# Two attention layers and an MLP on one core: order of SyncE's transfers, lag of the transposed scores, and halves of a projection in the first layer

## What is computed

```python
q = einsum('oc,bct->bot', Wq, x) + bq      # x, kv: (8, 256, 512); 16 heads of 16
k = einsum('oc,bct->bot', Wk, kv) + bk
v = einsum('oc,bct->bot', Wv, kv) + bv
attn = einsum('bhqd,bhdk->bhqk', q * scale, k)          # 512 x 512 for each head
attn = softmax(where(kv_mask, attn, -inf))
mean = attn @ v
std = sqrt(relu(attn @ (v * v) - mean * mean))
out = (instance_norm(x) * std + mean) * mask
```

## Time and profile before

| | |
|---|---|
| median of 3 runs | 1814.33 us (1808.19 to 1818.41) |
| the profiled execution | 1805.06 us, span 1803.3 us |
| TensorE matmuls | 1657.7 us busy, 92% |
| VectorE | 1279.9 us, 71% |
| ScalarE | 1065.6 us, 59% |
| GpSimd | 342.6 us, 19% |
| costliest group on VectorE | L598, 256 x 1222 ns |
| costliest group on ScalarE | L770, 256 x 1024 ns |

### The profile page before, as it was taken

How to read it: one execution, slowest core, us unless ns; L and a number is a source line. 1 busy time by engine, 2 the same in 40 slices (tenths; PEclk the granted TensorE clock), 3 DMA queues, 4 the chain that set the end, 5 groups by cost and what they waited for, 6 DMA issues and landing times.

```text
span 1803.3 us, 30832 instructions
## 1 busy us (share of the span) xinstructions
PE 1657.7 (92%) x10589; PEld 1124.1 (62%) x10589; DVE 1279.9 (71%) x2758; ACT 1065.6 (59%) x2351; POOL 342.6 (19%) x435
## 2 busy tenths in 40 slices
PE   6988888898888888899999989999999899999999
PEld 3333333333333334788878877888888788888888
DVE  2766867777777765798999889999999763232322
ACT  1556666666665565777877878888878752121111
POOL 0001111302111123232232222233322130000000
PEclk8999999999999999899999999999999899999999
DMA  5444453444444332233223434333333340000000
GB/s 181 138 137 136 143 153 96 144 119 137 122 125 140 112 123 69 84 74 81 69 68 102 113 87 124 89 89 89 92 93 83 88 129 13 1 24 1 24 17 19
DMA packets 108891, 167.97 MB, mean 93 GB/s; under 512 B 23616, under 2 KB 39360, under 8 KB 108608
## 3 DMA queue, kind: packets, MB, share of 16 engines
q1 hardware_dynamic: 96720, 140.74, 27.4%
q0 software_dynamic: 9472, 20.99, 4.6%
q10 hardware_dynamic: 2544, 4.26, 0.8%
HBM read 72.06 MB, written 34.60 MB: 59 GB/s over the span
## 4 chain that ended last, share of the span: by engine, by line
PE 53%; DVE 21%; SPq 8%; issue 7%; ACT 6%; DMA 4%; POOL 0%; ACTq 0%; DVEq 0%; POOLq 0%
PE ps L524 9%; PE ps L1928 9%; PE ps L1902 7%; PE ps L1251 4%; DVE at_t L1380 4%; DVE at_t L1385 4%; PE ps L1261 4%; PE ps L501 4%; SPq L298 3%; PE ps L510 3%; PE ps L1200 2%; PE ps L1907 2%; PE ps L478 2%; DMA ring<-top 2%; SPq L366 2%
## 5 line engine op out<-in xcount | busy, mean ns | idle before, releaser
L598 DVE TENSOR_REDUCE nmax<-ps 128x2 f32<-128x1024 f32 x256 | 310.9, 1222 | 159.6 <-PE ps L501 158.2
L770 ACT ACTIVATE prob<-ps 128x1024 f32<-128x1024 f32 x256 | 262.0, 1024 | 203.6 <-PE ps L510 198.7
L1588 ACT ACTIVATE at_prob<-at_t,at_nmax 128x256 f32<-128x256 f32 x512 | 256.5, 505 | 83.6 <-DVE at_nmax L1385 71.4
L524 PE MATMUL ps<-prob,v 128*64 128x512 f32 x1024 | 289.6, 644 | 4.0
L1385 DVE CUSTOM_DVE_ANT_0 at_t<-at_t,at_off 128x256 f32<-128x256 f32 x512 | 232.3, 490 | 8.8
L2087 DVE CAST mlp_h_hi<-mlp_h 128x512 fp32r<-128x512 f32 x64 | 28.4, 444 | 213.0 <-ACT mlp_h L1999 180.0
L1746 POOL TENSOR_TENSOR at_low<-at_low,at_high 128x512 fp32r<-128x512 f32 x64 | 87.2, 1362 | 471.6 <-DVE at_high L1414 471.6
L501 PEld LDWEIGHTS ps<-ring 64*128 64x128 f32 x512 | 49.6, 190 | 190.9 <-issue 149.4
L501 PE MATMUL ps<-ring 64*128 64x512 f32 x512 | 132.1, 513 | 35.2 <-issue 21.1
L1999 ACT ACTIVATE mlp_h<-ps,b 128x512 f32<-128x512 f32 x48 | 33.1, 690 | 218.3 <-PE ps L1902 218.3
L1200 PE MATMUL ps<-ident,at_prob 128*128 128x128 f32 x1024 | 157.3, 276 | 0.0
(11 more groups left out here) (215 smaller groups left out, 3850.4 us busy)
## 6 DMA issues: line engine op xcount, KB each, us to landing
ring<-rows SPq DMA_DIRECT2D x62, 512.0 KB, 4.8
rows<-shares_of SPq DMA_DIRECT2D x90, 256.0 KB
at_k_stack<-at_high SPq DMA_DIRECT2D x256, 64.0 KB, 2.5
at_q_stack<-at_high SPq DMA_DIRECT2D x128, 64.0 KB, 2.7
at_q_stack<-at_high POOLq DMA_DIRECT2D x128, 64.0 KB, 2.5
at_q_stack<-at_low SPq DMA_DIRECT2D x128, 64.0 KB, 2.1
at_k_stack<-at_low POOLq DMA_DIRECT2D x128, 64.0 KB, 2.3
c_in<-in_ctx SPq DMA_DIRECT2D x8, 512.0 KB, 4.6
```

The lines of the kernel that those rows point to most:

```text
L524: mm = eng.matmul(ps[2 * QD * k:2 * QD * (k + 1), VB, :], v[:, c, HG * G + 2 * p + k, :], prob[:, M % PROBS, k, :], start=(c == 0), stop=( ...
L598: eng.tensor_reduce(nmax[:, n % 2, j, 2 * p:2 * p + 2], ps[:, at:at + 2, :], AX, ALU.max, negate=True).then_inc(s_max, 1)
L770: eng.activation(prob[:, M % PROBS, :, :], ps[:, ST:ST + 2, :], ACT.Exp, scale=float(HD0) ** -0.5).then_inc(s_exp, 1)
L1588: ins = eng.activation(prob[:, m % 2, i, :], t[:, p, i, :], ACT.Exp, scale=-1.0, bias=nmax[:, m % 4, i:i + 1], accum_out=z[:, T % 2, j, 2 ...
```

## The change

On SyncE, `tops_in` comes first in each window, ahead of `shares_in` and of `regroup`. Its four DMAs count on two semaphores, so that `turned` waits for two heads at a time. LAG is 13, so the first `turned` of a group falls on step 5; `take_values` moves by one step with it. Both halves of the q projection are made at step 3 and of the k projection at step 6. At the start the constants of slot 0 are written first, those of slots 1 to 3 behind the first loads; then the rows of slot 1, the value weights and bias, and `ident` last.

```diff
-    LAG = 12
+    LAG = 13
...
-        if s in (2, 3, 5, 6) and w % 2 == 0 and w // 2 + 1 < PAIRS:
-            return [("q" if s < 4 else "k", w // 2 + 1, ((s + 1) % 3,))]
+        if s in (3, 6) and w % 2 == 0 and w // 2 + 1 < PAIRS:
+            return [("q" if s == 3 else "k", w // 2 + 1, (0, 1))]
...
-        def constants_out(k, src, done):
+        def constants_out(k, src, done, first, last):
             for i in range(2):
-                eng.dma_start(d["rows0"][k].rearrange("s p (i r) t -> i r (s p) t", i=2)[i, CONST:CONST + HD0],
-                              src[ROWS * i + CONST:ROWS * i + CONST + HD0, None, :].broadcast_to([HD0, 2 * RING, D]))\
-                   .then_inc(done, DMA)
+                eng.dma_start(d["rows0"][k, first:last].rearrange("s p (i r) t -> i r (s p) t", i=2)[i, CONST:CONST + HD0],
+                              src[ROWS * i + CONST:ROWS * i + CONST + HD0, None, :]
+                              .broadcast_to([HD0, 2 * (last - first), D])).then_inc(done, DMA)
...
-            constants_out(1, far, s_far_out)
+            constants_out(1, far, s_far_out, 0, RING if b else 1)
...
                 eng.dma_start(q_rows[at:at + 2, n % RING, h // 2, :].bitcast(F32),
-                              top[2 * h:2 * h + 2, n % 2, :].bitcast(F32)).then_inc(s_top, DMA)
+                              top[2 * h:2 * h + 2, n % 2, :].bitcast(F32)).then_inc(s_top[h // 2], DMA)
...
-        constants_out(0, scrap, s_const)
+        constants_out(0, scrap, s_const, 0, 1)
         far_out(0)
         rows_out("k", 0, (0,))
         rows_out("q", 0, (0,))
         for p in range(2):
             first_rows_in("k", p)
             first_rows_in("q", p)
-        eng.dma_start(ident[:], d["ident"]).then_inc(s_ident, DMA)
+        constants_out(0, scrap, s_const, 1, RING)
+        constants_out(1, far, s_far_out, 1, RING)
+        rows_out("k", 0, (1,))
+        rows_out("q", 0, (1,))
         eng.dma_start(w0[:, :, 2 * S:], d["w0"][:, :, 2 * S:]).then_inc(s_wv, DMA)
         eng.dma_start(bv0[:], d["bv0"]).then_inc(s_wv, DMA)
-        rows_out("k", 0, (1,))
-        rows_out("q", 0, (1,))
+        eng.dma_start(ident[:], d["ident"]).then_inc(s_ident, DMA)
...
         for w in range(GROUPS + 3):
             n, b, ahead = w - 2, w // NG - 1, w // 2 + 1
+            if 0 <= w - 1 < GROUPS:
+                tops_in(w - 1)
             if w % NG == 2 and b >= 0:
                 shares_in(b)
             if 0 <= n < GROUPS:
                 regroup(2 * n)
-            if 0 <= w - 1 < GROUPS:
-                tops_in(w - 1)
             lead(w, False)
...
-                    if M % 8 == 0:
-                        eng.wait_ge(s_top, HG * DMA * (M // 8 + 1))
+                    if M % 4 == 0:
+                        eng.wait_ge(s_top[M % 8 // 4], 2 * DMA * (M // 8 + 1))
...
-                if s in (0, 4) and 0 <= w - 2 < GROUPS:
+                if s in (1, 5) and 0 <= w - 2 < GROUPS:
                     take_values(2 * (w - 2) + s // 4)
```

More of the change, by code:

```diff
@@ L183, in layer0 @@
         s_out = {name: sem("rows_" + name) for name in "qk"}
-        s_top = sem("top")
+        s_top = [sem(f"top{p}") for p in range(2)]
         s_ring = {name: [sem(f"ring_{name}{k}") for k in range(RING)] for name in "qk"}
@@ L338, in constants_written @@
             if name == "q":
-                eng.wait_ge(s_const, 2 * DMA)
+                eng.wait_ge(s_const, 2 * DMA * (2 if n else 1))
             else:
-                eng.wait_ge(s_far_out, 2 * DMA * (n // NG + 1))
+                eng.wait_ge(s_far_out, 2 * DMA * (n // NG + (2 if n else 1)))
         def first_rows_in(name, p):
@@ L549, in tensor @@
                     scores(N)
-                if N < LAG:
+                if N < 12:
                     busy((0, 0, 3, 2, 0, 8, 0, 7, 0, 0, 1, 1)[N], VB, k_rows[:, 0, 0, :])
                 if 0 <= M < 8 * GROUPS:
-                    if M % 8 == 0:
-                        eng.wait_ge(s_top, HG * DMA * (M // 8 + 1))
+                    if M % 4 == 0:
+                        eng.wait_ge(s_top[M % 8 // 4], 2 * DMA * (M // 8 + 1))
                     if M:
@@ L634, in squares_of_x @@
             if b == 0 and h == 0:
-                eng.wait_ge(s_const, 2 * DMA)
+                eng.wait_ge(s_const, 4 * DMA)
             eng.tensor_tensor_reduce(scrap[:], X[:, b, h, :], X[:, b, h, :], 1.0, 0.0,
@@ L779, in masks @@
             if b:
-                eng.wait_ge(s_far_out, 2 * DMA * b)
+                eng.wait_ge(s_far_out, 2 * DMA * (b + 1))
             eng.wait_ge(s_mask, b + 1)
@@ L796, in take_turn @@
             if n >= 2:
-                eng.wait_ge(s_top, HG * DMA * (n - 1))
+                for p in range(2):
+                    eng.wait_ge(s_top[p], 2 * DMA * (n - 1))
             eng.activation(top[0:2 * HG, n % 2, :], ps[0:2 * HG, MB, :], ACT.Copy).then_inc(s_free, 1)
```

## The result

The change makes the kernel slower: median 1866.6 us (1860.4 to 1868.3) against 1814.6 beside it, ratio 1.028 with an interval of 1.025 to 1.032. The forecast, 1854, had the direction and the range; it was 12.6 us too low. The profiled execution took 1860.4 us, the lowest of its four. One of the ten executions of `e_start` (experiment 6) took 3861.4 us, in a slow state, and is left out of its median.

What follows compares the result with a forecast made beforehand. The chain from the maxima's copy over the k rows bounds odd windows, TensorE even ones. 19 + 4 + 13 - 4.5 + 0 + 9 = +40.5 gives 1845.6; the median, 9.3 higher, 1854; range 1828 to 1870.

Steps and rivals of the forecast that it cites:

- What bounds: First layer: a chain from the maxima's copy over the k rows' write and load ends odd windows; TensorE bounds even ones.
- Part 1, windows 3, 5, 9, ...: SyncE's queue, eight odd windows: regroup now delays the k rows, about 2.4 us each, +19 us (15 to 25).
- Part 1, windows 7, 11, ...: SyncE's queue, six odd windows already paying the regroup ahead of the maxima: +0.6 us each, +4 (0 to 14).
- Part 2: Even windows' heads: TensorE's clock low after the longer wait, nine more slow heads at 1.4 us, +13 (0 to 19).
- Rival (b): The chain is as worked out, but TensorE's clock stays at 2.4 GHz: 1841 us; chance 0.15.
- Part 3: Both projection halves in one step: half of the 8.8 us waits on VectorE saved, -4.5 us (-8.8 to 0).
- Part 4: Lag 13: one more step at the end, +1.7 us, against vanished stalls on the maxima: 0 (-3 to +3).
- Part 5: The start: `ident` queues behind constants, slot 1 rows and weights, landing at 38 us, not 28.4: +9 (-1 to +11).
- Rival (a): At the start `ident` is not late: 1844 us; chance 0.12.
- (c): Odd windows: the chain is not longer, as the k rows' 8.1 us shrink when started later: 1818 us; chance 0.08.
- (d): Odd windows: the stall on the maxima is the bound and the k rows land early enough: 1748 us; chance 0.03.
- (e): The change only removes TensorE's 33.3 and 8.8 us of stalls and nothing comes instead: 1772 us; chance 0.05.

Runs made afterwards that it cites:

- e_start: The kernel before with the new start alone (constants of slot 0 first, `ident` last): 1824.4 us, ratio 1.0045.
- experiment 6: The kernel before with the new start alone, measured at 1824.4 us (+9.0) and, once more for its trace, 1826.1 us (+11.9).
- experiment 1: The kernel before with `tops_in` moved ahead of `shares_in` and `regroup`, nothing else: 1859.3 us, ratio 1.026.
- experiments 1 and 2: The kernel before with maxima first alone, 1859.3 us; the changed kernel with regroup ahead of the maxima again, 1848.8 us.
- j_tops: The kernel before with maxima first on SyncE's queue alone, lag 12 and `take_values` unmoved: 1859.3 us, ratio 1.026.
- c_order: The changed kernel with SyncE's old order (`shares_in`, regroup, maxima), the rest as changed: 1848.8 us, ratio 1.020.
- d_filler: The changed kernel with 20 unread products ahead of the wait for the k rows in even windows from 4 on: 1840.6 us, ratio 1.016.
- g_qload: The changed kernel with k rows, then the q load, moved ahead of the regroup behind the maxima: 1813.3 us, ratio 0.999.

## Why the prediction was right, and where its sizes were not

- **What bounds.** Right. The chain from the maxima's copy over the k rows to the next scores decides the odd windows; the stalls on the maxima inside them were worth nothing by themselves (experiment 1).
- **Part 1, windows 3, 5, 9, ...: +19 forecast, +21.6 measured.** Right mechanism and place: k rows at copy + 6.0 (5.9), 18.3 to the next scores (17.9). Two edits remove the same cover; the forecast named both and costed one, which is how they act (experiments 1 and 2).
- **Part 1, windows 7, 11, ...: +4 forecast, +14.2 measured.** The step that failed is "I take +0.6 each": 2.4 each, at the upper bound. Maxima first alone gives 1.1 each (`j_tops`), the later `take_values` in the old order 1.6 (`c_order`). SyncE reaches the maxima 0.9 to 3.2 us after the copy, and the four DMAs then take 2.9 us instead of 2.5. I had named the slow issue behind long DMAs and then priced it near its lower end.
- **Part 2, clock: +13 forecast, about +24 with window 30,** beyond the upper bound of 19. Rival (b) is refuted by `d_filler` and by the slow first step of every head from window 4 on. The mis-sized terms: 1.4 us a head, read behind a wait of 1.78, was 2.1 (27.8 over 13 heads), because the low clock now lasts beyond the first step; and 12 of 14 heads were all of them, window 30's too. This is the largest of the errors.
- **Part 3, one step: -4.5 forecast, -10.3 measured,** beyond the lower bound of -8.8. The waits gave the half that was taken; "No work is removed" was the failing step: a projection without the break takes 0.21 us less, 5.9 in all.
- **Part 4: 0.** Odd heads and the tail gave -1.5 and -0.8, within the bounds.
- **Part 5: +9 forecast, +10.0 in the trace, 9.0 to 11.9 in experiment 6.** `ident` came at 40.0 (38). Rival (a) is refuted; and even with `ident` early the q rows are late next. The size was right, the way to it in part: I had `ident` wait in the queue behind the rows, but it landed 3.6 us after its issue, as before. What made it late is that SyncE came to issue it only at 36.4, behind 4.1 us of issue for the constants, 6.9 for the six row writes (5.4 in before) and 2.6 for the value weights and bias.
- **Rivals (c), (d), (e).** The k rows' 8.1 us to the load's issue stayed (8.4), so (c) falls; the 91.3 us before L503 refute (d) and (e).

The errors of the second, third and fourth term are +10, +11 and -6, so part of them cancelled, and three of the terms left their own bounds or reached them. By the traces the sum was 14.8 us short (40.5 against 55.3), by the medians 12.6. That 1866.6 still lies in the range is in part luck: its upper end was said to be the upper bounds of parts 1 and 2, but these come to 6 + 10 + 6 = 22 over 1854, which is 1876 and not 1870.

What is still open: why issuing six small DMAs behind 768 KB takes 4.7 us and not 3.3. The traces show it in more than one place, but no run changed the amount ahead of them alone; the expectation of `g_qload` speaks of a full queue, which no trace shows. The same holds for how the 0.21 us of a break come about.

## What to carry to other kernels

Before moving a transfer ahead on an in-order queue, list what it passes and ask of each whether the bound of the stage hangs on it: here the maxima passed the regroup, and the regroup thereby came ahead of the k rows, which set the window's end. A stall inside a window whose end is set by something else is slack; remove it and it returns in one piece at the end. Here the pieces of 5.4 to 7.0 us each cost TensorE its clock behind them, for 5.5 us in window 10. Work laid beside a wait (the regroup, beside SyncE's wait for the copy) is free only as long as both the order and the time of its input leave it there.

## What the runs showed of the hardware that I had not expected

- TensorE took 0.21 us longer for a projection cut in two: 1.59 us for six 128x512 products in a row, 1.80 for two groups of three.
- Twenty useless products in front of a wait made the kernel 24 us faster (ratio 1.016 instead of 1.028), by holding the granted clock at 1.00 in the steps behind it at 11 of 14 heads.
- SyncE's issue of the same six small DMAs lasts 3.3 us, 4.7 behind three row writes and 5.7 behind the constants.
